# A decoder kernel on one Trainium2 core: setup moved into the fill, attention semaphores in two sets, and a reordered Mamba round

## The chip, the cores and the metric

The kernel runs on one core of one Trainium2 chip. The metric is the device time of one execution in microseconds (us); lower is better. The kernel before took 7854.28 us, the median of three runs (7828.51 to 7878.61).

The profile calls the engines PE (matrix multiply, with PEld for its weight loads), DVE (vector), ACT (scalar, activation functions), POOL (the second vector-like engine) and SP (which here issues DMAs). Every engine works through its own program in order and waits on semaphores that others raise.

## The reference, cut to what matters

The input `x` is 64 sequences of 128 tokens by 128 features (float32, 4.19 MB), with a context of 64 x 77 x 128 and a mask. Two decoder layers are computed in six stages: four Mamba layers, a cross attention, a mixture of experts, a trajectory step, a decoder block, and a last cross block. Some 45% of the time goes to the Mamba stage, which the change touches most. One of its layers computes

```
residual = hidden + residual;  h = layernorm(residual) * w + b
xin, z   = split(h @ in_w.T);  u = silu(causal_conv(xin) + cb)
dtr, B, C = split(u @ xp_w.T); dt = softplus(dtr @ dtp_w.T + dtp_b)
for each of 16 states n:  s_n[t] = exp(dt*A_n)[t] * s_n[t-1] + (dt*u*B_n)[t]
y = sum_n C_n * s_n + D*u;     hidden = (y * silu(z)) @ out_w.T
```

A is stored as a logarithm, so the kernel needs the exponential of it, negated (`a_neg`).

## The kernel before, in words

**Mamba stage** (`mamba_stage`, lines 97 to 763). The 64 sequences are 16 groups of four; a round does one group of one layer, so there are 64 rounds. A round runs three groups at once: the 16 scans of the present group, the last steps of the group behind (its gate, its output product, its new residual), and the first steps of the group ahead (norm, convolution, silu, projections, dt). Each round is one block of the five engine programs (line 594), which ends when all engines are through; two sets of semaphores take turns (`Turns`), and SP clears the other set at the start of a block.

*DVE* scans state after state: `dve_scan` (L422) needs the decay of that state from ACT and the input term `dBu` from POOL. The scan of a state read out on DVE (eleven of them) goes in place into PSUM, and `dve_read_out` (L439) multiplies it by C. For states 1, 5, 8, 10 and 13 the scan goes to plain memory (SBUF) and POOL reads it out (L450). Between scans DVE does the gate of the group behind after scan 1 (L337), the mean and variance of the group ahead after scan 3 (`Pre.dve`, L199 and L202), and three steps of softplus after scans 8, 9 and 11.

*ACT* makes the decays: `act_da(n+1, n)` writes the decay of state n+1 during step n, into one of two PSUM places that alternate with n; it waits until state n-1 has been scanned and read out. Each is a small column of zeros (L390) and two exponentials (L393). Between them stand, in this order: after the decay of state 3, the silu block (two silus of the convolution, L249, a wait for the gate, two silus of z, L319); after the decay of state 5, the copy of x's projection (`act_x`, L260) and of the new residual (`act_new`, L353); after the decay of state 6 the variance (`act_var`, L213 and L214); later softplus, the normalised tokens (L219) and their transposed copy (L231). Silu, exponential and logarithm are in different function tables, so a table load stands where the kind changes.

*PE* sums the read-out states into two PSUM banks by products with the identity (L467), which DVE's next read-out into the same buffer waits for. Its order at the start of a round:

```
behind.pe_late_sums; ahead.pe_conv(1); wait gate; sum(0); ahead.pe_z; sum(1); ahead.pe_x; behind.pe_out; sum(2); sum(3)
```

`pe_z` (L313) waits for the silus of the convolution, `pe_x` (L255) for those and for z's first silu, and `pe_out` (L343, L347) makes the residual that `act_new` copies.

*POOL* makes `dBu` (L408), two states ahead of the scan, and reads out its five states. *SP* loads rows of B and C, the residuals, and stores.

In a layer's first round (shape 0) DVE also copies `w_out` (L683) and builds the skip matrices (L495), and in its 15th (shape 14) it builds the next layer's convolution weights (L488 to L491).

**Before the first round** three blocks run one after the other. The first (L2844) issues 15 DMAs, 13 of them copies from DRAM to DRAM (the residual stream, its padding, a padded copy of `x`, of the context and of the mask), and waits for all. The second (L167) sets buffers to zero on DVE. The third (L507, the fill) loads the first weights, and runs the first steps for two groups.

**The attention stages** (`xattn_stage`, `trajectory_stage`, `decoder_stage`) run 19, 18 and 19 rounds, each a block. They have one set of semaphores (`Sems`): after each block SP clears it (L66) and a barrier of all engines follows (L67).

Of the kernel before, what the change touches and what calls it, by code (L numbers as in the profile page):

```python
# [16 lines left out]
P = 128  # L17
BATCH, SEQ, D = 64, 128, 128
GB = 4
# [17 lines left out]
LATE = 2  # L37
HCD = (2, 0, 1, 2, 0, 1, 2, 0, 1, 0, 1)
# [58 lines left out]
def mamba_stage(nc, w, consts, res, bc_dram):  # L97
# [9 lines left out]
    with ExitStack() as ctx:  # L107
# [26 lines left out]
        var, rstd, shift = (sb(n, [P, GB]) for n in ("var", "rstd", "shift"))  # L134
# [3 lines left out]
        ab, ey, ln1, small = (sb(n, [P, CH, TOK]) for n in ("ab", "ey", "ln1", "small"))  # L138
        dt, dtu, u, zg = (pair(n, [P, CH, TOK]) for n in ("dt", "dtu", "u", "zg"))
# [27 lines left out]
        with nc.Block() as block:  # L167
            @block.vector
            def _(dve):
                nc.vector.memset(h_ch[:], 0.0)  # L170
                nc.vector.memset(zeros[:], 0.0)
                nc.vector.memset(small_at[:], SMALL_Y)
                nc.vector.memset(poly_at[:], -0.75 * THIRD)
                nc.vector.memset(eps_at[:], LN_EPS)
                nc.vector.memset(xp[2 * DS:2 * DS + DR + 1, :], 1.0)
                nc.vector.memset(u[1][:], 0.0)
                nc.vector.memset(zg[1][:], 0.0)
                for part in hcd + hcp:
                    nc.vector.memset(part[:], 0.0)
                nc.vector.memset(w_out[:], 0.0)  # L180
                nc.vector.memset(bank[:, B_DA:8], 0.0)

        s = Turns(nc, ctx, ["mb_" + n for n in [
            "res", "rp", "store", "rows", "b0", "b1", "b2", "b3", "c0", "c1", "c2", "c3",
            "stats", "var", "norm", "xh", "tr", "h", "conv", "u", "xp", "xps", "dtp", "abs", "ey", "sq", "small", "ln", "poly", "log", "dt", "dtu", "z", "zg",
            "dbu", "da", "scan", "hcd", "hcp", "sumd", "sump", "late", "yg", "out", "new", "raw", "weights", "wb", "skip", "wo", "apos", "aneg"]])

        class Pre:
# [5 lines left out]
            def load(self, sp, g):  # L194
                sp.dma_start(r_tok[:], tile_rows(res, g)).then_inc(s["mb_res"], 16)
# [166 lines left out]
        class Scan:  # L362
# [17 lines left out]
            def act_da(self, act, m, j):  # L380
                q = self.q if m < DS else self.next_q
                n = m % DS
                if j >= 1:
# [6 lines left out]
                nc.scalar.activation(da_of(n)[:, :, 0:1], zeros[:], ACT.Copy)  # L390
                for c in range(CH):
                    k = c * DS + n
                    e = nc.scalar.activation(da_of(n)[:, c * GB:(c + 1) * GB, 1:],  # L393
# [17 lines left out]
            def dve_scan(self, dve, n):  # L411
# [10 lines left out]
                nc.vector.tensor_tensor_scan(flat(to), flat(da_of(n)), flat(dBu[n % RING][:]), 0.0,  # L422
# [62 lines left out]
        def dve_weights(dve):  # L485
            dve.wait_ge(s["mb_raw"], 5 * 16)
            for k in range(DC):
                nc.vector.tensor_tensor(w_conv[:, k, :], w_u[:], conv_row[:, k, :], ALU.mult)  # L488
            nc.vector.tensor_copy(w_x[:], x_raw[:])
            nc.vector.tensor_copy(conv_b[:], vec[:, CB:CB + CH])  # L490
            nc.vector.tensor_copy(norm_wb[:], vec[:, NW:NW + 2]).then_inc(s["mb_wb"], 1)  # L491

        def dve_skip(dve):
            for c in range(CH):
                m = nc.vector.tensor_scalar(skip[:, c], ident[:], vec[:, DD + c:DD + c + 1], None, ALU.mult)  # L495
            m.then_inc(s["mb_skip"], 1)
# [2392 lines left out]
```

## Time and profile before

| | |
|---|---|
| median of three runs | 7854.28 us |
| the profiled execution, its own time | 7862.71 us |
| its span, first to last instruction | 7860.9 us |
| mean granted TensorE clock in it | 0.841 |

| engine | busy us | share of the span |
|---|---|---|
| PE | 6285.0 | 80% |
| DVE | 6331.9 | 81% |
| ACT | 4396.8 | 56% |
| POOL | 4934.3 | 63% |

A share of busy time is an average over stages with different limits, so the stages are read one by one. The page cuts the span into 40 slices; in the first 19, some 3,730 us, which is the Mamba stage, DVE stands at 9 (90% or more) in all but the first slice, and the other engines below it or, POOL, beside it. A timeline lists instructions in order of time, with the idle time of the engine ahead of them and who ended it.

### The profile page before, as it was taken

The numbers are of one execution on the slowest core, as the hardware profiler recorded it, in microseconds if no ns is written. First come the engines' busy times: TensorE is split into PE (matmuls) and PEld (weight loads), VectorE is DVE, ScalarE is ACT, GpSimd is POOL, SyncE is SP. The second block draws the span as 40 slices with busy tenths as digits, with TensorE's granted clock in tenths as the row PEclk, the third lists the DMA queues.
The fourth block names the chain that finished last, engine by engine and source line by source line (L and its number), as shares of the span: only waits on it lengthen the run. The fifth ranks groups of instructions, "written<-read, shape, count | busy, mean of one in ns | idle before, by whom it ended". The sixth has DMA issues, their size and how long they took to land. (4 is left out here: it accounts for less than half of the span.)

```text
span 7860.9 us, 92400 instructions
## 1 busy us (share of the span) xinstructions
PE 6285.0 (80%) x25986; PEld 3332.1 (42%) x26001; DVE 6331.9 (81%) x14154; ACT 4396.8 (56%) x8495; POOL 4934.3 (63%) x3020
## 2 busy tenths in 40 slices
PE   5888888988888988888798777777557777777745
PEld 2333333333333333333455545555334554545522
DVE  4999999999999999999555488888666666666557
ACT  3666666766666666766455434444225555555533
POOL 4999999998999989999322176666123444344300
PEclk9999999999999999999767788888557777777755
DMA  4444444444444444434101077776110000000011
GB/s 169 172 158 171 164 167 154 173 155 164 165 159 170 159 176 156 173 156 168 50 22 28 18 231 220 223 216 197 45 34 11 7 9 10 10 10 10 7 38 35
DMA packets 373862, 896.52 MB, mean 114 GB/s; under 512 B 28169, under 2 KB 270214, under 8 KB 307110
## 3 DMA queue, kind: packets, MB, share of 16 engines
q1 hardware_dynamic: 332646, 692.64, 24.0%
q0 software_dynamic: 40960, 201.36, 8.9%
q14 instruction: 204, 1.67, 0.1%
q8 instruction: 52, 0.85, 0.0%
HBM read 850.57 MB, written 56.77 MB: 115 GB/s over the span
## 5 line engine op out<-in xcount | busy, mean ns | idle before, releaser
L408 POOL TENSOR_TENSOR mb_dBu<-mb_dtu,mb_rows_b 128x1024 f32<-128x1024 f32 x1026 | 2398.5, 2362 | 74.5 <-DVE mb_bank L422 41.0
L422 DVE TENSOR_TENSOR_SCAN mb_bank<-mb_bank,mb_dBu 128x1024 f32<-128x1024 f32 x704 | 1608.7, 2285 | 92.5 <-PEq L594 49.6
L467 PE MATMUL mb_bank<-mb_hcd,ident 128*128 128x512 f32 x2560 | 1232.0, 612 | 105.9 <-DVE mb_hcd L439 98.9
L393 ACT ACTIVATE mb_bank<-mb_dt,mb_a_neg 128x508 f32<-128x508 f32 x2050 | 1311.1, 670 | 1.5
L450 POOL TENSOR_TENSOR mb_hcp<-mb_hs,mb_rows_c 128x1024 f32<-128x1024 f32 x320 | 753.5, 2355 | 221.4 <-DVE mb_hs L422 221.4
L439 DVE TENSOR_TENSOR mb_hcd<-mb_bank,mb_rows_c 128x1024 f32<-128x1024 f32 x704 | 861.8, 1224 | 31.4
L467 PEld LDWEIGHTS mb_bank<-mb_hcd,ident 128*128 128x128 f32 x2560 | 474.1, 195 | 758.8 <-issue 509.0
L422 DVE TENSOR_TENSOR_SCAN mb_hs<-mb_bank,mb_dBu 128x1024 f32<-128x1024 f32 x320 | 729.6, 2280 | 0.0
L1588 POOL DMA_INDIRECT ex_rows<-in_ex_table,ex_idx x512 | 492.0, 961 | 330.7 <-issue 169.0
L467 PE MATMUL mb_bank<-mb_hcp,ident 128*128 128x512 f32 x1024 | 544.9, 659 | 140.2 <-POOL mb_hcp L450 139.3
L390 ACT ACTIVATE mb_bank<-mb_zeros 128x8 f32<-128x8 f32 x1025 | 176.0, 172 | 755.5 <-DVE mb_hcd L439 330.2
L1080 PE MATMUL de_bank<-ident,de_a_e 128*128 128x128 f32 (+1 forms) x2048 | 370.2, 340 | 211.0 <-DVE de_a_e L1196 210.9
L242 PE MATMUL mb_bank<-mb_h_ch,mb_w_conv 128*128 128x512 f32 x1048 | 474.2, 594 | 0.9 <-ACT mb_h_ch L231 0.9
L1037 POOL TENSOR_TENSOR de_a_e<-de_a_sp,de_a_m 128x1024 f32<-128x1024 f32 x128 | 245.0, 1914 | 332.9 <-DVE de_a_m L1182 179.5
L1080 PEld LDWEIGHTS de_bank<-ident,de_a_e 128*128 128x128 f32 (+1 forms) x2048 | 300.6, 180 | 264.6 <-DVE de_a_e L1196 239.7
L467 PEld LDWEIGHTS mb_bank<-mb_hcp,ident 128*128 128x128 f32 x1024 | 199.4, 202 | 435.0 <-issue 218.9
L1150 ACT ACTIVATE de_a_pt<-de_bank 128x512 f32<-128x512 f32 (+1 forms) x512 | 280.8, 591 | 122.6 <-PE de_bank L1080 122.5
L1182 DVE MAX8 de_a_m<-de_a_sp 128x8 f32<-128x128 f32 x1024 | 210.1, 277 | 143.7 <-ACT de_a_sp L1135 71.0
L1565 PE MATMUL ex_bank<-ex_w_sim,ex_xT 128*128 128x512 f32 x512 | 257.6, 644 | 80.9 <-PEq L67 74.4
L1672 ACT ACTIVATE ex_dg_in<-ident,ex_lin 128x128 f32<-128x128 f32 x512 | 156.5, 388 | 295.5 <-DVE ex_lin L1707 295.5
L242 PEld LDWEIGHTS mb_bank<-mb_h_ch,mb_w_conv 128*128 128x128 f32 x1048 | 198.8, 190 | 257.1 <-issue 255.8
L1642 PE MATMUL ex_bank<-ex_rows,ex_dg_in 128*128 128x256 f32 x1024 | 291.0, 448 | 0.0
(372 smaller groups left out, 12903.1 us busy)
## 6 DMA issues: line engine op xcount, KB each, us to landing
mb_rows_b<-bc_rows SPq DMA_DIRECT2D x259, 1024.0 KB, 7.0
mb_rows_c<-bc_rows SPq DMA_DIRECT2D x258, 1024.0 KB, 6.7
stream<-mb_r_post SPq DMA_DIRECT2D x69, 256.0 KB, 2.4
mb_r_tok<-stream SPq DMA_DIRECT2D x67, 256.0 KB, 2.7
mb_r_old<-stream SPq DMA_DIRECT2D x65, 256.0 KB, 2.8
ex_rows<-in_ex_table,ex_idx POOLq DMA_INDIRECT x512, 5.5
tj_x_tok<-stream SPq DMA_DIRECT2D x17, 256.0 KB, 3.0
bc_rows<-mb_xp SPq DMA_DIRECT2D x65, 64.0 KB, 2.1
```

What stands on the lines that cost most here:

```text
L242: m = nc.tensor.matmul(bank[:, M0 + c], w_conv[:, k, c * P:(c + 1) * P], h_ch[:, :, k:k + SEQ], start=(k == 0), stop=(k == DC - 1))
L393: e = nc.scalar.activation(da_of(n)[:, c * GB:(c + 1) * GB, 1:], dt[q][:, c].rearrange("p (b t) -> p b t", b=GB)[:, :, 1:], ACT.Exp, scale ...
L408: nc.gpsimd.tensor_tensor(by_c(dBu[m % RING][:]), by_c(chains(dtu[q][:])), over_c(rows_b[:, n]), ALU.mult).then_inc(s["mb_dbu"], 1)
L422: nc.vector.tensor_tensor_scan(flat(to), flat(da_of(n)), flat(dBu[n % RING][:]), 0.0, ALU.mult, ALU.add).then_inc(s["mb_scan"], 1)
L439: nc.vector.tensor_tensor(by_c(hcd[HCD[k]][:]), by_c(da_of(n)), over_c(rows_c[:, n]), ALU.mult).then_inc(s["mb_hcd"], 1)
L450: nc.gpsimd.tensor_tensor(by_c(hcp[(k + self.q) % 2][:]), by_c(hs[k % 2][:]), over_c(rows_c[:, n]), ALU.mult).then_inc(s["mb_hcp"], 1)
L467: m = nc.tensor.matmul(bank[:, B_Y + c], ident[:], part[:, c * GB:(c + 1) * GB], start=(n == 0), stop=False)
L1080: m = self.nc.tensor.transpose(self.bank[0:nk, 4 + j, h * P:(h + 1) * P], self.e_of(t, nk)[:, 4 * j + h], self.ident[:])
L1150: self.nc.scalar.activation(self.pt[t % 2][0:nk, 4 * j:4 * j + 4].rearrange("p h q -> p (h q)"), self.bank[0:nk, 4 + j], ACT.Copy).then_in ...
L1565: nc.tensor.matmul(bank[:, j], xT[q][:, b], w_sim[:, 4 * j:4 * j + 4], start=True, stop=True).then_inc(p["sim"], 1)
L1588: nc.gpsimd.indirect_dma_start(rowsb[b][:, h], None, w["table"], bass.IndirectOffsetOnAxis(idx[b][:, h:h + 1], 0)).then_inc(got[b], 16)
L1642: m = nc.tensor.matmul(bank[:, HID, 0:FI], dg_in[:, h], rowsb[k % GB][:, h, IB:IB + FI], start=False, stop=(h == PH - 1))
```

## The change

**Setup.** The first block keeps only two DMAs (identity and head mask). The other 13 are issued in the fill: four of them (`early`, 9.4 MB: the stream, its padding, `x`) behind the weight loads, nine (`late`, 4.0 MB) behind the load of the third group; the fill's end waits for all. The block of memsets is gone; DVE clears what is needed at the start of the fill, and the rest behind the convolution weights. The first groups are loaded from `x` itself. PE's first product, with a zeroed `u`, becomes one with a zeroed buffer, further back.

**Semaphores.** The three attention stages use `Turns`: SP clears the other set at the start of a block, and the clear and the barrier behind each block are gone. The decoder's loop of 13 rounds becomes one of six pairs, with one more round behind it.

**Norm statistics.** `Pre.dve` and `act_var` leave the rounds. ACT sums the four sequences in step 14 (four copies with a running sum, one small scaling) and, in step 0 of the next round, sums their squares about the mean (four squares, one small step).

**PE.** `pe_z` goes ahead of the wait for the gate and of `sum(0)`.

**Scan 4.** Its decay is made in step 2, ahead of the silu block, without a wait, into `ey` in SBUF; step 3 makes none.

**Weights.** `w_out`, the skip matrices and the small copies go to ACT (steps 5 and 9 of the rounds concerned); the convolution weights stay on DVE, in step 12, with one operand copied to PSUM by ACT (step 11).

```
+            def act_sums(self, act, there):
+                act.wait_ge(s["mb_res"], there)
+                for b in range(GB):
+                    m = nc.scalar.activation(xh[:, b], r_tok[:, b], ACT.Copy, accum_out=sums[:, b:b + 1])
+                m.then_inc(s["mb_sums"], 1)
+                act.wait_ge(s["mb_sums"], 1)
+                nc.scalar.activation(shift[:], sums[:], ACT.Copy, scale=-1.0 / D).then_inc(s["mb_mean"], 1)
+            def act_squares(self, act):
+                for b in range(GB):
+                    m = nc.scalar.activation(xh[:, b], r_tok[:, b], ACT.Square, bias=shift[:, b:b + 1],
+                                             accum_out=squares[:, b:b + 1])
+                m.then_inc(s["mb_squares"], 1)
+                act.wait_ge(s["mb_squares"], 1)
+                nc.scalar.activation(var[:], squares[:], ACT.Identity, bias=eps_at[:, 0:1], scale=1.0 / D).then_inc(s["mb_var"], 1)
...
             def act_da(self, act, m, j):
-                if j >= 1:
+                if m == EARLY:
+                    pass
+                elif j >= 1:
...
+                da = early_da if n == EARLY else da_of(n)
...
             def _(act):
-                        scan.act_da(act, n + 1, n)
+                        if n + 1 != EARLY:
+                            scan.act_da(act, n + 1, n)
                         if n == 2:
+                            scan.act_da(act, EARLY, n)
                             for c in range(CH):
                                 ahead.act_conv(act, c, 1)
...
-                        if n == 5:
-                            pre.act_var(act)
+                        if n == 0:
+                            pre.act_squares(act)
+                        if n == 5 and shape == 0:
+                            act.wait_ge(s["mb_out"], 1)
+                            nc.scalar.activation(w_out[:], out_raw[:], ACT.Copy).then_inc(s["mb_wo"], 1)
+                            act_skip(act)
...
+                        if n == 14:
+                            pre.act_sums(act, 16)
...
             def _(dve):
-                        if n == 6 and shape == 0:
-                            nc.vector.tensor_copy(w_out[:], out_raw[:]).then_inc(s["mb_wo"], 1)
-                        if n == 6 and shape == GROUPS - 2:
-                            dve.wait_ge(s["mb_xp"], 1)
-                            dve_weights(dve)
-                        if n == 6 and shape == 0:
-                            dve_skip(dve)
-                        if n == 3:
-                            pre.dve(dve)
+                        if n == 12 and shape == GROUPS - 2:
+                            dve.wait_ge(s["mb_wu"], 1)
+                            dve_weights(dve, bank[:, M1, 0:DI])
...
             def _(pe):
                     behind.pe_late_sums(pe)
                     ahead.pe_conv(pe, 1)
+                    ahead.pe_z(pe)
                     pe.wait_ge(s["mb_yg"], 1)
                     scan.pe_sum(pe, 0)
-                    ahead.pe_z(pe)
                     scan.pe_sum(pe, 1)
...
             @block.sync
             def _(sp):
-                pre.load(sp, 1)
+                pre.load(sp, x_in, 0)
                 load_raw(sp, 0)
                 load_used(sp, 0)
+                moves = early(sp, s["mb_moved"])
                 sp.wait_ge(s["mb_xh"], 1)
...
+                moves += late(sp, s["mb_moved"])
...
+                sp.wait_ge(s["mb_moved"], 16 * moves)
...
 # in each of the three attention stages
-        s = Sems(nc, st, [...])
+        s = Turns(nc, st, [...])
         def round_of(i, shape):
+            s.use(shape % 2)
                 def _(sp):
+                    s.clear_other()
-            s.clear()
```

## Rows read from the trace of the kernel before

**Rows 1.** Busy us (instructions) of PE, PEld, DVE, ACT, POOL; clock; DMA share; GB/s.
```profile
1000.00:2000.00 1000.00, 883.83 (x2120) 366.39 (x2118) 963.91 (x692) 668.54 (x1224) 913.99 (x421) 0.96 0.42 161
```

**Rows 2.** DVE timeline of two rounds: start, duration, instruction, idle before it.
```profile
2000.10 2.30 DVE L422 TENSOR_TENSOR_SCAN mb_bank<-mb_bank,mb_dBu 128x1024 f32<-128x1024 f32 x1 [0.69 <-PEq L594]
...
2015.68 2.30 DVE L422 TENSOR_TENSOR_SCAN mb_bank<-mb_bank,mb_dBu 128x1024 f32<-128x1024 f32 x1 [0.54 <-ACT mb_bank L393]
...
2021.35 2.27 DVE L422 TENSOR_TENSOR_SCAN mb_bank<-mb_bank,mb_dBu 128x1024 f32<-128x1024 f32 x1
...
2056.57 2.30 DVE L422 TENSOR_TENSOR_SCAN mb_bank<-mb_bank,mb_dBu 128x1024 f32<-128x1024 f32 x1 [0.76 <-PEq L594]
...
2070.28 0.86 DVE L199 BATCH_NORM_STATS2 mb_stats<-mb_r_tok 128x6 f32<-128x128 f32 x4
...
2071.52 2.27 DVE L422 TENSOR_TENSOR_SCAN mb_bank<-mb_bank,mb_dBu 128x1024 f32<-128x1024 f32 x1
...
2077.16 2.27 DVE L422 TENSOR_TENSOR_SCAN mb_bank<-mb_bank,mb_dBu 128x1024 f32<-128x1024 f32 x1
```

**Rows 3.** ACT timeline of the same two rounds.
```profile
2019.38 1.28 ACT L393 ACTIVATE mb_bank<-mb_dt,mb_a_neg 128x508 f32<-128x508 f32 x2
...
2042.32 1.65 ACT L219 ACTIVATE mb_xh<-mb_r_tok,mb_shift,mb_rstd 128x128 f32<-128x128 f32 x4 [2.29 <-POOL mb_shift L209]
...
2052.38 0.18 ACT L390 ACTIVATE mb_bank<-mb_zeros 128x8 f32<-128x8 f32 x1 [2.05 <-DVE mb_hcd L439]
...
2060.16 0.18 ACT L390 ACTIVATE mb_bank<-mb_zeros 128x8 f32<-128x8 f32 x1 [2.23 <-DVE mb_hcd L439]
...
2062.36 0.18 ACT L390 ACTIVATE mb_bank<-mb_zeros 128x8 f32<-128x8 f32 x1 [0.80 <-DVE mb_hs L422]
...
2063.77 1.28 ACT L249 ACT_TABLE_LOAD   x1
...
2074.22 0.60 ACT L353 ACTIVATE mb_r_post<-mb_bank 128x512 f32<-128x512 f32 x1 [1.30 <-PE mb_bank L347]
```

**Rows 4.** PE timeline of the same two rounds.
```profile
2000.11 3.25 PE L331 MATMUL mb_bank<-mb_hcp,ident 128*128 128x512 f32 x4 [2.12 <-PEq L594]
...
2056.62 1.96 PE L331 MATMUL mb_bank<-mb_hcp,ident 128*128 128x512 f32 x4 [2.24 <-PEq L594]
...
2063.56 1.91 PE L467 MATMUL mb_bank<-mb_hcd,ident 128*128 128x512 f32 x4
2065.81 1.99 PE L313 MATMUL mb_bank<-mb_h_ch,mb_w_z 128*128 128x512 f32 x4 [0.33 <-ACT mb_u L249]
2067.63 1.88 PE L467 MATMUL mb_bank<-mb_hcp,ident 128*128 128x512 f32 x4
```

**Rows 5.** POOL timeline of the second of these rounds.
```profile
2064.72 11.62 POOL L408 TENSOR_TENSOR mb_dBu<-mb_dtu,mb_rows_b 128x1024 f32<-128x1024 f32 x5
```

**Rows 6.** DVE timeline, work on weights: in the fill, then beside POOL in rounds.
```profile
66.11 1.43 DVE L488 TENSOR_TENSOR mb_w_conv<-mb_w_u,mb_conv_row 128x256 f32<-128x256 f32 x4 [3.27 <-DMA mb_conv_row<-in_mb_conv_row]
...
1053.21 1.54 DVE L683 COPY mb_w_out<-mb_out_raw 128x256 f32<-128x256 f32 x1
1054.67 2.58 DVE L495 TENSOR_SCALAR mb_skip<-ident,mb_vec 128x128 f32<-128x128 f32 x2
...
3668.37 3.48 DVE L488 TENSOR_TENSOR mb_w_conv<-mb_w_u,mb_conv_row 128x256 f32<-128x256 f32 x4 [1.42 <-DMA mb_conv_row<-in_mb_conv_row]
```

**Rows 7.** Timeline of the start, DVE and SP (SPq issues DMAs).
```profile
46.12 0.49 DVE L170 MEMSET mb_h_ch<- 128x524 f32 x1 [45.25 <-PEq L2844]
...
58.69 0.40 SPq L195 DMA_DIRECT2D mb_r_tok<-stream  x1
...
117.96 2.30 DVE L422 TENSOR_TENSOR_SCAN mb_bank<-mb_bank,mb_dBu 128x1024 f32<-128x1024 f32 x1 [13.73 <-PEq L507]
```

**Rows 8.** SP's releases by a block's end (L1343) and the barrier (L67), 3776 to 3791.
```profile
L1343 SPq EVENT_SEMAPHORE  x1: 17/17/17, 3786.6 to 3786.6; - x1
...
L67 SPq EVENT_SEMAPHORE  x2: 17/17/17, 3778.9 to 3787.0; - x2
```

More of the change, by code:

```diff
@@ L133, in mamba_stage @@
         mv = sb("mv", [P, GB, 2])
-        var, rstd, shift = (sb(n, [P, GB]) for n in ("var", "rstd", "shift"))
+        var, rstd, shift, sums, squares = (sb(n, [P, GB]) for n in ("var", "rstd", "shift", "sums", "squares"))
         xh = sb("xh", [P, GB, D])
@@ L165, in mamba_stage @@
         y_psum, x_psum = bank[:, B_Y:B_Y + CH], bank[:, M0:M0 + CH]
[L167 to L181, printed above, removed]
         s = Turns(nc, ctx, ["mb_" + n for n in [
             "res", "rp", "store", "rows", "b0", "b1", "b2", "b3", "c0", "c1", "c2", "c3",
-            "stats", "var", "norm", "xh", "tr", "h", "conv", "u", "xp", "xps", "dtp", "abs", "ey", "sq", "small", "ln", "poly", "log", "dt", "dtu", "z", "zg",
-            "dbu", "da", "scan", "hcd", "hcp", "sumd", "sump", "late", "yg", "out", "new", "raw", "weights", "wb", "skip", "wo", "apos", "aneg"]])
+            "init", "blank", "moved", "stats", "sums", "mean", "squares", "var", "norm", "xh", "tr", "h", "conv", "u", "xp", "xps", "dtp", "abs", "ey", "sq", "small", "ln", "poly", "log", "dt", "dtu", "z", "zg",
+            "dbu", "da", "scan", "hcd", "hcp", "sumd", "sump", "late", "yg", "out", "new", "raw", "weights", "copies", "wu", "wb", "skip", "wo", "apos", "aneg"]])
         class Pre:
@@ L580, in _ @@
                 first.pe_dt(pe, False)
+                pe.wait_ge(s["mb_blank"], 1)
+                for c in range(CH):
+                    nc.tensor.matmul(bank[:, B_Y + c], ident[:], hcd[HCD[-1]][:, c * GB:(c + 1) * GB], start=True, stop=False)
                 first.pe_dt(pe, True)
@@ L1515, in experts_stage @@
         p = Prefixed(s, "ex_")
-        got = [st.enter_context(nc.semaphore(f"ex_got{b}")) for b in range(GB)]
+        got = consts["got"]
         w_sim = sb("w_sim", [P, 2 * PH, NK])
@@ L2463, in _ @@
                             n4.dve_done(dve)
-            s.clear()
         for i in (-2, -1, 0):
             round_of(i, i)
-        with nc.Fori(1, GROUPS - 2) as i:
-            round_of(i, 1)
-        for i in range(GROUPS - 2, GROUPS + 1):
+        with nc.Fori(0, (GROUPS - 4) // 2) as pairs:
+            for q in range(2):
+                round_of(pairs * 2 + 1 + q, 1 + q)
+        for i in range(GROUPS - 3, GROUPS + 1):
             round_of(i, i)
+        s.clear()
 def decoder_host(i):
@@ L2843, in build @@
         loaded = st.enter_context(nc.semaphore("consts_loaded"))
+        consts["got"] = [st.enter_context(nc.semaphore(f"ex_got{b}")) for b in range(GB)]
         with nc.Block() as block:
@@ L2862, in _, with early, late @@
                 nc.vector.memset(consts["half_neg"][:], -0.5)
[L2863 removed]
+        def early(sp, sem):
+            copies = [(after_mamba, a["x"]), (padded[0:TOK], a["x"][0:TOK]), (padded[TOK * (GROUPS + 1):], a["x"][0:3 * TOK]),
+                      (x_ahead[0:BATCH * SEQ], a["x"])]
+            for dst, src in copies:
+                sp.dma_start(dst, src).then_inc(sem, 16)
+            return len(copies)
+        def late(sp, sem):
+            copies = [(stream[k][TOK * GROUPS:], a["x"][0:TOK]) for k in range(1, 5)]
+            copies += [(x_ahead[BATCH * SEQ:], a["x"][0:TOK])]
+            for whole, src in ((ctx_ahead, a["ctx"]), (mask_ahead, a["mask"])):
+                copies += [(whole[0:BATCH], src), (whole[BATCH:], src[0:GB])]
+            for dst, src in copies:
+                sp.dma_start(dst, src).then_inc(sem, 16)
+            return len(copies)
+        mamba_stage(nc, of("mb"), consts, a["x"], padded, bc_dram, early, late)
         xattn_stage(nc, of("xa"), consts, x_ahead, padded[TOK:TOK * (GROUPS + 2)], ctx_ahead, mask_ahead, stream[1][0:TOK * GROUPS])
```

91 lines of the change are left out of this document (56 added, 35 removed).

## The prediction, made before the changed kernel was run

> **What bounds the kernel now.** I read the page's 40 slices first: in the Mamba slices DVE is full. The windows view confirms it for one stretch: DVE is busy 964 of 1,000 us, POOL 914, at a granted clock of 0.96 [rows 1]. Then I read the DVE timeline of two neighbouring rounds [rows 2]. DVE runs without a gap, with two exceptions: about 0.7 us at the start of a round, and in one round of two 0.54 us ahead of scan 4, which the trace puts down to ACT's decay. So what DVE no longer does is worth its time only as far as the next decay is there. I therefore followed the decays on ACT [rows 3] and, behind them, PE's order [rows 4]. Times below are from a round's first scan; the plain round starts at 2056.57, the stalled one at 2000.10.
>
> **The round: what is taken off DVE.** From the norm's first row to scan 4 is 2071.52 - 2070.28 = 1.24 us, which goes; the 0.54 us stall in every second round goes too, since scan 4's decay is early. Scan 4 could start at 13.71. If nothing else held DVE that would be 1.24 + 0.27 = 1.51 us a round.
>
> **The round: what ACT and PE do instead.** The new sums and squares cover four tiles of 128x128; the nearest row, four tokens' normalisation, is 1.65 us [rows 3]. The running sum's own price isn't in the trace: I bound it by 0 and by a doubling to 3.3, and take the lower end, nearest to the row. Either way it lies in ACT's waits: 2.23 us ahead of the second decay, 2.05 us ahead of the last decay of a round, with 0.8 us more ahead of the third decay. Without that cover it would cost up to 1.9 us each. The added waits on its own two semaphores hold only the next decay, inside the same gaps.
>
> The early decay is another matter. It stands in front of the silu block, behind decay 3, whose start to the table load is 2063.77 - 2062.36 = 1.41 us. That is what one more decay adds. z's product now starts at 2065.81 - 2056.57 = 9.24; it becomes 9.24 + 1.4 = 10.64. PE has meanwhile nothing to do: the convolution ends at about 7.0 (start of sum 0, 2063.56), and sum 0, which filled this gap, now stands behind z. Sum 0 takes 1.81 (sum 1's start less z's is 1.82 for the same number of passes). From z's start to the start of the residual's copy is 2074.22 - 2065.81 = 8.41 us, through sum 1, x's projection and the output product. With sum 0 added, that copy starts at 10.64 + 8.41 + 1.81 = 20.86 instead of 17.65.
>
> **Who waits for it.** ACT is in order: the decay for scan 6 stands behind that copy, 0.60 + 1.28 = 1.88 us later. So scan 6 cannot start before 20.86 + 1.88 = 22.74. It starts now at 2077.16 - 2056.57 = 20.59 in the plain round and at 21.25 in the stalled one, where DVE itself was the limit. So **scan 6 becomes the stall**: +2.15 and +1.49, mean +1.82 us a round, after DVE has given up everything that the norm gave it. Behind scan 6 the work is unchanged in order and amount on all engines (softplus hangs on the same PE chain and shifts with it), so nothing is paid back: 64 x 1.82 = +116 us.
>
> **The clock.** In the stalled round PE's first group takes 3.25 us where the plain one takes 1.96 [rows 4]: the half level (1.2 GHz) after 2.12 us of idleness; after 2.24 us in the other round it did not fall. PE now idles 10.64 - 7.0 = 3.6 us ahead of z, and what follows is the chain to scan 6. The price per round lies between 0 and 2 x 1.29 (z and sum 0 both at half rate). I take 1.29 in every second round, as often as the slow group comes now: 64 x 0.65 = +42 us.
>
> **Scan 4's operands.** Its decay and its `dBu` are now both in SBUF. The trace shows what such work costs beside POOL [rows 6]: four products take 1.43 us in the fill and 3.48 us in a round; a copy takes 1.54, two scalings 2.58. POOL runs five `dBu` back to back from 8.15, 2.32 us each [rows 5], so one ends at 8.15 + 3 x 2.32 = 15.11; if scan 4 has to wait for that, it starts 1.40 late and ends at 17.4, and scan 5 ends by 20.9, still ahead of 22.74. The stall covers it: 0. POOL would lose 2.3 us there, and its next `dBu`, for scan 7, is then ready at 19.8, in time. The Trainium skill ("SBUF — State Buffer", section "Who interferes with whom") says that a DVE instruction with two SBUF inputs and a GpSimd instruction that reads SBUF lock each other out for the whole instruction, which speaks against this step; by that rule the forecast's sum stays as it is, and only the third rival's changes.
>
> **Special rounds.** In a layer's first round 1.54 + 2.58 = 4.1 us leave DVE; in its 15th 1.42 of waiting and 3.48, against 1.43 that come back in step 12 (one operand in PSUM, so at the fill's price): 3.5. Both lie behind scan 6, so they count in full: 4 x 7.6 = -30 us. ACT's share (some 1 us) has its slack ahead of decays 7 and 13.
>
> **The fill.** The first scan starts at 117.96; the fill's first issue stands at 58.69, after 46 us of copies and the memsets [rows 7]. The copies moved 13.4 MB (sizes in the code), so 0.30 MB per us. After, the fill starts at about 4 us, an estimate from the two small loads that remain. By its own steps it would end at 4 + 59 = 63, a gain of 55. But the queue holds 9.4 MB from about 9.5, so to 41; the store of B and C's rows queues behind it, then five row loads of 1 MB and 4.0 MB late: 41 + 9.3/0.30 = 72, and 3 to land: 75. SP's wait for the late copies holds the end of the block and so all engines. I take -43 us, from -55 (hidden) to -28 (if everything late waits for the last row).
>
> **Semaphore sets.** From a block's release to the barrier's is 3787.0 - 3786.6 = 0.4 us [rows 8]; with 56 rounds, three clears staying, 53 x 0.4 = -21. SP's clear at the start delays loads that are needed a round later: 0. The decoder's longer loop body I put at 0: the trace doesn't price it, and the other two stages already have loops of pairs. Bounds -25 and 0.
>
> **Sum.** +116 + 42 - 30 - 43 - 21 = +64. Against the profiled execution, 7862.7, that gives 7927; its own time stands 8.4 above the median of the runs, 7854.3, so the forecast is **7918 us**, +0.8%.
>
> **Rivals.** (A) PE stays at full clock: without the 42, +22, so 7876. For it: the 2.24 us gap that did nothing. (B) PE falls in every round: 64 x 1.29 = 83 instead of 42, +105, so 7959; for it, the new gap is longer than either of those seen. With two slow groups it would be +188, 8042, the far end. (C) **Faster**: the residual's copy does not catch scan 6, and DVE's relief sets the round. It decides at a copy that starts by about 17.5 (scan 6 would come at 13.71 + 5.64 = 19.35, less 1.88). Then 64 x 1.51 = -97, in all -191: 7663. With scan 4 held by POOL for 1.40 each round it is -101: 7753. DVE's work on weights shows such waits [rows 6], so I put C at 7753. It is also what the rule of the Trainium skill named above would give. Against C: PE's program puts sum 0 and sum 1, 3.6 us, between z and that copy, and 20.86 is over 3 us late. That the change doesn't do what it says has no place apart: the norm's DVE instructions are simply gone.
>
> **Chances.** Forecast 0.42, A 0.21, B 0.23, C 0.14. A measurement of this kernel tells about 1% (79 us) from no change: faster means under 7776, slower over 7933. C gives 0.14 faster. Of the forecast, with the fill's and the sets' bounds (about 40 us either way), 0.4 lies above 7933, and of B 0.8: 0.17 + 0.18, slower 0.35; the rest, 0.51, within 1%. The range leaves out C and the far end of B, and reaches from A less the fill's bound to B plus the sets': 7820 to 8010. The likeliest case alone is 7880 to 7960.
>
> **What would show it.** DVE's timeline: no norm rows, scan 4 between 13.7 and 15.2, and scan 6 at 22.5 to 24, its idle ended by ACT's decay (L393's line); the residual's copy near 20.9, its idle ended by PE's output product; z at 10.6 with PE idle ahead of it; rounds of 58 us and more. The first scan near 75. If scan 6 comes at 19.4 to 20.7 without idle, C holds, and the in-order reading of ACT or PE is wrong. If scan 4 lasts 2.3 us with its start at 13.7, the lock does not touch it.

## The result and the profile after

The changed kernel takes **7938.63 us** (median of 7 runs, 7907.57 to 7962.75) against 7854.28 (7 runs beside it): the ratio is **1.0108**, 95% interval 1.0077 to 1.0138. It is slower, 20.6 us above the forecast and inside the range. The profiled execution took 7962.26 us, with a span of 7960.0, 99.1 more than before.

Where the 99.1 us are, by the span's stages: the fill saves 44.75 (first scan at 73.21, before 117.96), the Mamba rounds take 163.6 more (first scan to last instruction, 3650.1 to 3813.7), and the attention stages save 20.6 (cross attention +13.0, the trajectory stage -6.6, the decoder -27.0). The last 0.9 us lie in the other stages and between stages.

The windows view of the kernel after, same columns and same stretch as [rows 1], and the page's first line:

```profile
1000.00:2000.00 1000.00, 849.53 (x2029) 349.60 (x2029) 915.84 (x521) 688.76 (x1446) 907.13 (x402) 0.96 0.39 153
```
```profile
PE 6311.9 (79%) x25986; PEld 3329.5 (42%) x26001; DVE 6321.1 (79%) x13608; ACT 4597.7 (58%) x9561; POOL 5057.2 (64%) x3020
```

DVE was 964 us busy in these 1,000 and is 916 now, since a round takes longer; its work has hardly become less. Over the whole span its busy time fell from 6331.9 us to 6321.1 only: the norm and the weights freed some 109 us, and the scans take 87 us more, about 80 of them in scan 4, as the next rows show. The DVE timeline of a round at full clock, first scan at 2333.96, answers to the second half of [rows 2]: scan 0, scans 4 and 5, and scan 6.

```profile
2333.96 2.30 DVE L428 TENSOR_TENSOR_SCAN mb_bank<-mb_bank,mb_dBu 128x1024 f32<-128x1024 f32 x1 [1.05 <-PEq L622]
...
2347.68 3.57 DVE L428 TENSOR_TENSOR_SCAN mb_bank<-mb_ey,mb_dBu 128x1024 f32<-128x1024 f32 x1
...
2352.42 2.28 DVE L428 TENSOR_TENSOR_SCAN mb_hs<-mb_bank,mb_dBu 128x1024 f32<-128x1024 f32 x1
2356.59 2.30 DVE L428 TENSOR_TENSOR_SCAN mb_bank<-mb_bank,mb_dBu 128x1024 f32<-128x1024 f32 x1 [1.90 <-ACT mb_bank L398]
```

Scan 4 starts 13.72 after scan 0 and waits for nothing that the profile names, but lasts 3.57 us, where it lasted 2.27. Scan 6 comes at 22.63, behind 1.90 us of idleness that ACT's decay ends. Now ACT and PE in the same round, answering to [rows 3] and [rows 4]: the squares, the early decay into `mb_ey`, the table load behind it, the residual's copy; z ahead of sum 0.

```profile
2335.20 0.39 ACT L212 ACTIVATE mb_xh<-mb_r_tok,mb_shift 128x128 f32<-128x128 f32 x1
2335.49 0.19 ACT L212 ACTIVATION_READ_ACCUMULATOR mb_xh<-mb_r_tok,mb_shift 128x1 f32 x1
...
2337.55 0.18 ACT L395 ACTIVATE mb_bank<-mb_zeros 128x8 f32<-128x8 f32 x1 [0.39 <-DVE mb_hcd L445]
...
2341.18 1.31 ACT L398 ACTIVATE mb_ey<-mb_dt,mb_a_neg 128x508 f32<-128x508 f32 x2
2342.51 1.28 ACT L251 ACT_TABLE_LOAD   x1
...
2354.68 0.60 ACT L355 ACTIVATE mb_r_post<-mb_bank 128x512 f32<-128x512 f32 x1 [2.25 <-PE mb_bank L349]
```
```profile
2344.55 1.98 PE L315 MATMUL mb_bank<-mb_h_ch,mb_w_z 128*128 128x512 f32 x4 [1.72 <-ACT mb_u L251]
2346.37 1.88 PE L473 MATMUL mb_bank<-mb_hcd,ident 128*128 128x512 f32 x4
2348.09 1.88 PE L473 MATMUL mb_bank<-mb_hcp,ident 128*128 128x512 f32 x4
```

In another round (first scan at 1321.58) PE has waited 3.47 us ahead of z. The granted clock of the four microseconds behind that wait is 0.50, the half level of 1.2 GHz (windows view, columns as in [rows 1]); z takes 3.78 us, sum 0 3.08, the copy starts at 23.68, and scan 6 at 25.59 after 4.82 us of idleness:

```profile
1332.16 3.78 PE L315 MATMUL mb_bank<-mb_h_ch,mb_w_z 128*128 128x512 f32 x4 [3.47 <-ACT mb_u L251]
1335.74 3.08 PE L473 MATMUL mb_bank<-mb_hcd,ident 128*128 128x512 f32 x4
...
1338.66 1.88 PE L473 MATMUL mb_bank<-mb_hcp,ident 128*128 128x512 f32 x4
```
```profile
1332.00:1336.00 4.00, 3.83 (x5) 1.77 (x6) 3.96 (x3) 1.30 (x4) 4.00 (x3) 0.50 0.00 0
```
```profile
1347.17 2.30 DVE L428 TENSOR_TENSOR_SCAN mb_bank<-mb_bank,mb_dBu 128x1024 f32<-128x1024 f32 x1 [4.82 <-ACT mb_bank L398]
```

At the start, SP and DVE, answering to [rows 7]: the first group's load, the last of the late copies, the first scan.

```profile
3.46 0.38 SPq L181 DMA_DIRECT2D mb_r_tok<-in_x  x1
...
61.03 1.50 SPq L2914 DMA_DIRECT2D mask_ahead<-in_mask  x2
```
```profile
73.21 2.30 DVE L428 TENSOR_TENSOR_SCAN mb_bank<-mb_bank,mb_dBu 128x1024 f32<-128x1024 f32 x1 [21.98 <-PEq L516]
```

### The profile page after: what moved, and what is told of

Same layout as the page of the kernel before. It is cut to its first block and busy times, and to the rows that moved or that the text cites. A ratio compares the mean times of both kernels' runs of the same rounds, so it can differ in the third digit from the quotient of the medians.

```text
span 7960.0 us, 92226 instructions
## 1 busy us (share of the span) xinstructions
PE 6311.9 (79%) x25986; PEld 3329.5 (42%) x26001; DVE 6321.1 (79%) x13608; ACT 4597.7 (58%) x9561; POOL 5057.2 (64%) x3020
## 5 line engine op out<-in xcount | busy, mean ns | idle before, releaser
L413 POOL TENSOR_TENSOR mb_dBu<-mb_dtu,mb_rows_b 128x1024 f32<-128x1024 f32 x1026 | 2520.7, 2479 | 101.4 <-DVE mb_bank L428 59.7
L428 DVE TENSOR_TENSOR_SCAN mb_bank<-mb_bank,mb_dBu 128x1024 f32<-128x1024 f32 x640 | 1464.6, 2288 | 266.4 <-ACT mb_bank L398 185.4
L398 ACT ACTIVATE mb_bank<-mb_dt,mb_a_neg 128x508 f32<-128x508 f32 x1922 | 1230.0, 671 | 1.5
L473 PE MATMUL mb_bank<-mb_hcp,ident 128*128 128x512 f32 x1024 | 494.5, 605 | 103.8 <-POOL mb_hcp L456 103.8
L315 PE MATMUL mb_bank<-mb_h_ch,mb_w_z 128*128 128x512 f32 x260 | 169.7, 786 | 175.5 <-ACT mb_u L251 175.5
L1081 POOL TENSOR_TENSOR de_a_km<-de_kT,hmask 128x308 f32<-128x308 f32 x64 | 64.4, 1006 | 374.2 <-PE de_bank L1096 374.1
```

The lines of the kernel that those rows point to most:

```text
L398: e = nc.scalar.activation(da[:, c * GB:(c + 1) * GB, 1:], dt[q][:, c].rearrange("p (b t) -> p b t", b=GB)[:, :, 1:], ACT.Exp, scale=a_neg ...
L413: nc.gpsimd.tensor_tensor(by_c(dBu[m % RING][:]), by_c(chains(dtu[q][:])), over_c(rows_b[:, n]), ALU.mult).then_inc(s["mb_dbu"], 1)
L428: nc.vector.tensor_tensor_scan(flat(to), flat(da), flat(dBu[n % RING][:]), 0.0, ALU.mult, ALU.add).then_inc(s["mb_scan"], 1)
L473: m = nc.tensor.matmul(bank[:, B_Y + c], ident[:], part[:, c * GB:(c + 1) * GB], start=(n == 0), stop=False)
```

## The experiments

My theory: of the parts in the rounds, the two changes of order cost the time (z ahead of sum 0, scan 4's decay ahead of the silu block), through the chain PE, residual's copy, decay of scan 6; the clock adds to it; the rest of the change gains. The rivals were that the norm statistics on ACT, or the lock between DVE and POOL, make the rounds longer.

In the table, "round" is the mean length of the 52 ordinary rounds (all but a layer's first, 15th and 16th), and scan 4, scan 6 and the residual's copy are typical starts in a round, all in us from the profile of each kernel. The ratio, with its 95% interval, is to runs of the kernel before that were made beside that kernel; their medians lie between 7831.94 and 7863.23 us, so kernels are compared by their ratios.

| kernel | median us | ratio | round | scan 4 | scan 6 | copy |
|---|---|---|---|---|---|---|
| before | 7854.28 | | 56.21 | 14.95, 15.58 | 20.59, 21.25 | 17.65 |
| after | 7938.63 | 1.0108 (1.0077 to 1.0138) | 59.11 | 13.71 | 22.63 | 20.72 |
| z_back | 7787.43 | 0.9906 (0.9871 to 0.9941) | 56.54 | 13.71 | 20.92 | 19.00 |
| decay_back | 7853.93 | 0.9990 (0.9965 to 1.0016) | 57.48 | 14.55 | 21.28 | 19.37 |
| both_back | 7768.50 | 0.9896 (0.9864 to 0.9928) | 55.90 | 14.55 | 20.22 | 17.65 |
| z_alone | 7901.83 | 1.0063 (1.0041 to 1.0086) | 57.49 | 14.95 | 21.28 | 19.37 |
| busy_pe | 7896.50 | 1.0058 (1.0037 to 1.0078) | 58.25 | | 22.63 | |
| norm_back | 7764.61 | 0.9870 (0.9829 to 0.9911) | 56.20 | 14.95 | 20.58 | |
| best | 7857.49 | 1.0014 (0.9995 to 1.0033) | 57.64 | 13.71 | 19.37 | 17.31 |
| best_norm | 7948.90 | 1.0094 (1.0063 to 1.0126) | 58.85 | 14.94 | 20.58 | |

**The two changes of order.** `z_back` is the kernel after with z behind sum 0 again:

```
                     ahead.pe_conv(pe, 1)
-                    ahead.pe_z(pe)
                     pe.wait_ge(s["mb_yg"], 1)
                     scan.pe_sum(pe, 0)
+                    ahead.pe_z(pe)
```

> The changed kernel with one edit undone: z's product stands behind sum 0 again. Theory 1 (in-order chain: scan 6 waits for ACT's decay, which stands behind the residual's copy, which waits for PE's output product): the copy comes 1.8 us earlier, at about 18.9 instead of 20.7 from the round's start, scan 6 at 20.7 to 20.9 (then scan 5's end is the limit, as scan 4 still lasts 3.6), the plain round 56.2 to 56.6 instead of 58.1, and PE's gap ahead of z is half as long, so few or no slow groups there: 7938 less 118 to 180, so 7760 to 7820. Theory 2 (the lock between scan 4 and POOL costs the time): scan 4 and POOL are as before, so rounds stay near 58 and the time at 7900 or more.

`decay_back` keeps z ahead and makes scan 4's decay as the others are, in PSUM, behind the silu block (`da_of(n)` in place of `early_da`, in the scan too):

```
-                        if n + 1 != EARLY:
-                            scan.act_da(act, n + 1, n)
+                        scan.act_da(act, n + 1, n)
                         if n == 2:
-                            scan.act_da(act, EARLY, n)
```

> The changed kernel with one edit undone: scan 4's decay is made behind the silu block, in PSUM; z stays ahead of sum 0. Theory 1: z starts 1.4 us earlier, at 9.2, the residual's copy at about 19.4, scan 6 at 21.3 to 21.4 with 1 us of idle ahead of it, the plain round about 56.8: 7938 less 80 to 130, so 7810 to 7860. Theory 2: with the lock gone scan 4 lasts 2.3, scan 6 comes at 20.2 without idle, rounds of 55.6, and the time is about 7710.

`both_back` has both edits.

> The changed kernel with both edits undone: z behind sum 0, scan 4's decay behind the silu block in PSUM. Theory 1: the residual's copy at 17.65 in the plain round as before the change, scan 4 at 14.6 behind its decay (0.8 idle), scan 6 at about 20.2 without idle, plain round 55.4; where PE starts slow, the stall at scan 4 comes back (15.6) and the round is 56.4: a mean gain of 0.2 to 0.5 us a round over the kernel before, with the special rounds, the fill and the sets 7735 to 7765. Theory 2 gives the same here. If the running sums on ACT cost time in the round (a third theory), it stays above 7800.

`z_alone` is the other way about: the kernel before, with `ahead.pe_z(pe)` ahead of the wait for the gate and of `sum(0)`, and nothing else.

> The kernel before with one edit of the change alone: z's product ahead of sum 0. Theory 1 (in-order chain through the residual's copy): the copy comes 1.8 us later, at about 19.4, and scan 6 at 21.3 instead of 20.6, as in the run with the decay put back; rounds of 57.1 and, where PE is slow behind its gap, more: about 7850 plus 60 to 90, so 7910 to 7940. A rival (this edit is free or gains the 0.54 us stall of every second round, and only the early decay costs): 7830 to 7850.

DVE in `z_back` (scan 4, scan 6; first scan at 2232.77), in `decay_back` (first scan at 2271.45), in `both_back` (scans 4, 5 and 6; first scan at 2266.91) and in `z_alone` (scan 6; first scan at 2324.83):

```profile
2246.48 3.57 DVE L428 TENSOR_TENSOR_SCAN mb_bank<-mb_ey,mb_dBu 128x1024 f32<-128x1024 f32 x1
...
2253.69 2.30 DVE L428 TENSOR_TENSOR_SCAN mb_bank<-mb_bank,mb_dBu 128x1024 f32<-128x1024 f32 x1 [0.18 <-ACT mb_bank L398]
```
```profile
2286.00 2.30 DVE L426 TENSOR_TENSOR_SCAN mb_bank<-mb_bank,mb_dBu 128x1024 f32<-128x1024 f32 x1 [0.75 <-ACT mb_bank L396]
...
2292.73 2.30 DVE L426 TENSOR_TENSOR_SCAN mb_bank<-mb_bank,mb_dBu 128x1024 f32<-128x1024 f32 x1 [0.98 <-ACT mb_bank L396]
```
```profile
2281.47 2.30 DVE L426 TENSOR_TENSOR_SCAN mb_bank<-mb_bank,mb_dBu 128x1024 f32<-128x1024 f32 x1 [0.76 <-ACT mb_bank L396]
...
2284.94 2.28 DVE L426 TENSOR_TENSOR_SCAN mb_hs<-mb_bank,mb_dBu 128x1024 f32<-128x1024 f32 x1
2287.14 2.27 DVE L426 TENSOR_TENSOR_SCAN mb_bank<-mb_bank,mb_dBu 128x1024 f32<-128x1024 f32 x1
```
```profile
2346.11 2.30 DVE L422 TENSOR_TENSOR_SCAN mb_bank<-mb_bank,mb_dBu 128x1024 f32<-128x1024 f32 x1 [0.61 <-ACT mb_bank L393]
```

The idleness ahead of scan 6 is 1.90 us with both, 0.98 with z ahead alone, 0.18 with the early decay alone, and none with neither. By the ratios, z ahead costs 0.9% while the decay is late (0.9896 to 0.9990; on the kernel before, 0.6%), and 2.0% beside the early decay (0.9906 to 1.0108). The early decay costs 1.2% while z is ahead, and nothing that can be told (0.9896 against 0.9906, the intervals overlap) while sum 0 fills PE's gap. The two delays of the copy simply add: the early decay's 1.35 us (17.65 to 19.00) and z's 1.72 (to 19.37) make 3.07 (20.72). Time is lost only by what reaches scan 6 as a wait, so the second delay costs more than the first. Undoing both takes 2.1% off: the theory stands, and what remains of the change makes the kernel 1.0% faster. Two sizes were missed: `z_alone` took less than the 7910 to 7940 us expected, though clearly more than the rival's 7830 to 7850, and `both_back` came out just above its range.

**The clock.** `busy_pe` is the kernel after with two of the convolution's four products of the second half made twice, so that PE's wait ahead of z, up to 3.5 us in ordinary rounds, is at most 1.8 us in 61 of the 64 rounds:

```
+                    for k in range(2):
+                        nc.tensor.matmul(bank[:, 1], w_conv[:, k, P:2 * P], h_ch[:, :, k:k + SEQ], start=(k == 0), stop=(k == 1))
                     ahead.pe_conv(pe, 1)
                     ahead.pe_z(pe)
```

> The changed kernel with two products of the convolution made twice, in the gap in which PE waits for the silus, so that PE idles 1.8 instead of 3.6 us there. Theory 1 with the clock as a second cost: z keeps its place at 10.6, the copy at 20.7, scan 6 at 22.6 in nearly every round, and the 25 rounds in which scan 6 waited longer (62 us more in all in the profiled execution) become plain ones: 7938 less 40 to 60, so about 7880 to 7900, still slower than the kernel before. If those longer waits are not from PE's clock after its idleness, the time stays at 7938 or grows by what PE does more.

PE in `busy_pe` (first scan at 2302.10) and its scan 6:

```profile
2307.36 1.88 PE L739 MATMUL mb_bank<-mb_h_ch,mb_w_conv 128*128 128x512 f32 x4
2309.08 3.60 PE L244 MATMUL mb_bank<-mb_h_ch,mb_w_conv 128*128 128x512 f32 x8
2312.68 1.99 PE L315 MATMUL mb_bank<-mb_h_ch,mb_w_z 128*128 128x512 f32 x4
```
```profile
2324.73 2.30 DVE L428 TENSOR_TENSOR_SCAN mb_bank<-mb_bank,mb_dBu 128x1024 f32<-128x1024 f32 x1 [1.88 <-ACT mb_bank L398]
```

More work for PE, and less time: the ratio falls from 1.0108 to 1.0058, 0.5% or 39 us, and scan 6 stands at 22.63 in nearly every round. In the kernel after, 25 of 64 rounds have 3.3 to 4.8 us of idleness ahead of scan 6; what they have above the usual 1.9 sums to 62 us, and 3 such rounds remain here. Those 25 are among the 31 rounds in which PE has waited 3.3 us or more ahead of z; behind the other six of these waits, and behind the 33 waits of 2.0 us or less, z ran at full rate. These 33 are rounds in which PE's first group was slow already (2.98 us in the round at 2333.96), so that the convolution ended later and the wait became shorter. The length of the wait alone thus doesn't tell whether the clock falls. In `decay_back` PE waits 2.0 to 2.1 us ahead of z in 40 rounds, and z was slow (2.9 to 3.7 us) in 20 of them: part of what z ahead costs by itself is the clock, too.

**The lock.** `pool_holds` is the kernel after, in which POOL begins the `dBu` of scan 6 only when scan 4 is done, so nothing on POOL reads SBUF beside scan 4:

```
-                    pool.wait_ge(s["mb_scan"], m - RING + 1)
+                    pool.wait_ge(s["mb_scan"], 5 if m == 6 else m - RING + 1)
```

> The changed kernel, with POOL's product for scan 6 waiting until scan 4 is done, so that POOL stands idle when scan 4 starts. If scan 4's 3.57 us are a wait for POOL's running instruction plus 2.29 of work, it lasts 2.3 now, and scan 5 ends 1.3 earlier; scan 6 stays at 22.6, since it waits for ACT, and the time stays at 7938. If two SBUF operands make the scan itself slower, it stays at 3.57. If the lock had a part in scan 6's wait, rounds fall below 58 and the time to 7860.

DVE's scan 4 and scan 6 in `pool_holds` (first scan at 2329.72):

```profile
2343.43 2.29 DVE L428 TENSOR_TENSOR_SCAN mb_bank<-mb_ey,mb_dBu 128x1024 f32<-128x1024 f32 x1
...
2352.35 2.30 DVE L428 TENSOR_TENSOR_SCAN mb_bank<-mb_bank,mb_dBu 128x1024 f32<-128x1024 f32 x1 [3.17 <-ACT mb_bank L398]
```

The same scan of the same two SBUF operands takes 2.29 us without POOL and 3.57 beside it, and the 1.28 us saved there stand again ahead of scan 6 (3.17 for 1.90). The time is 7945.33, ratio 1.0108 (1.0075 to 1.0140): the wait of scan 4 for POOL is real and cost the changed kernel nothing.

**The norm statistics.** `norm_back` is `both_back` with the statistics on DVE and the variance on ACT in step 5, as before; the sums and squares on ACT leave the rounds:

```
                         if n == 3:
+                            pre.dve(dve)
...
-                        if n == 0:
-                            pre.act_squares(act)
-                        if n == 14:
-                            pre.act_sums(act, 16)
```

> The kernel with both edits undone, and the norm's statistics on DVE again in the rounds (rows behind scan 3, variance on ACT in step 5). Theory 1: scan 4 was waiting for its decay at 14.55, so DVE's 1.24 us of statistics fill most of that wait: scan 4 at 14.95, round 56.1 instead of 55.7 in plain rounds, no change in slow ones: 7768 plus 15 to 30, so 7780 to 7800. If what DVE no longer does is worth its full 1.24 us a round: 7768 plus 79, so about 7847.

The round grows by 0.30 us, as expected, and the Mamba stage of the profile by 14.6, but the total doesn't show it: 7764.61 lies below the 7780 to 7800 expected and below `both_back`, and the intervals overlap. Moving the statistics buys next to nothing here.

**The attention stages' sets.** `xa_one_set` is `both_back` with cross attention on one set, a clear and a barrier behind each block (`Sems` for `Turns`, no `use` or `clear_other`, `s.clear()` in the loop); `xa_after` is the same edit on the kernel after, and `xa_before` gives cross attention alone two sets in the kernel before.

```
-        s = Turns(nc, st, ["xa_" + n for n in [
+        s = Sems(nc, st, ["xa_" + n for n in [
...
-            s.use(shape % 2)
...
-                    s.clear_other()
...
+            s.clear()
```

> The kernel with both edits undone, and the cross attention's semaphores in one set again, with the clear and the barrier behind each block. If a release costs 0.4 us, as the trace of before shows, the cross attention takes 7 us more than with two sets (733 in the run with both edits undone, 720 to 724 in the others), so 727 to 741. A rival, from the stages' times (710 before the change, 720 to 734 with two sets): the two sets themselves made this stage slower, and it comes back to about 710.

> The changed kernel with the cross attention's semaphores in one set again. If two sets are what lengthens this stage: it takes 668 to 711 us, as in the three runs with one set, instead of 719 to 734, as in the seven with two, and less of it lies at the half clock level (285 to 392 us instead of 443 to 476); the whole about 7938 less 15 to 50. If the stage's time only depends on when it starts: anywhere between 668 and 734.

> The kernel before, with two sets of semaphores in the cross attention alone. If two sets are what lengthens this stage: 719 to 734 us instead of 710, with 440 us or more of it at the half level, and the whole 10 to 20 us longer than before. If a clear and a barrier less simply saves 0.4 us a round, as predicted: 703.

Totals: 7755.92, ratio 0.9867 (0.9832 to 0.9901); 7947.09, ratio 1.0150 (1.0114 to 1.0187); 7862.01, ratio 1.0040 (1.0019 to 1.0061). The stage itself took 695.8, 681.9 and 701.6 us, against 710.1 before and 723.1 after. It fits no theory of the sets: one set spans 668 (`z_alone`) to 710, two sets 682 (`best`) to 734 (`both_back`). What goes along with the stage's length is the time that PE spends in it at the half level: 285 us in `z_alone`, 392 before, 449 after, 476 in `both_back`. The windows of the stage, before and after (columns as in [rows 1]), show the same instruction counts at a granted clock of 0.72 and 0.69:

```profile
3771.00:4482.00 711.00, 610.68 (x4608) 397.25 (x4608) 380.71 (x1237) 372.00 (x768) 194.94 (x240) 0.72 0.10 26
```
```profile
3890.00:4613.00 723.00, 632.47 (x4608) 409.93 (x4608) 381.46 (x1237) 371.70 (x768) 194.79 (x240) 0.69 0.09 25
```

In `xa_one_set` and `xa_after` the stage is 38 and 41 us shorter than in the kernels that they change, but the decoder, whose code is the same, is 35 and 27 us longer (1714.5 for 1679.4, 1705.9 for 1679.2), and the whole span changed by +4 and -9 us only. Whether the sets move the clock stays open, and so does why the whole of `xa_before` is 0.4% longer than the kernel before beside it.

**An attempt at the gain.** `best` is `z_back` with `pool_holds`' wait and with sum 1 behind the output product, to keep the early scan 4 and give scan 6 its decay in time; `best_norm` puts the statistics back on DVE, as in `norm_back`.

```
                     behind.pe_out(pe)
+                    scan.pe_sum(pe, 1)
```

> The changed kernel with three edits that follow from the runs so far: z behind sum 0, sum 1 behind the output product, and POOL's product for scan 6 waiting for scan 4. Theory 1: the residual's copy comes at about 17.2 instead of 19.0 (z behind sum 0), scan 4 lasts 2.3, scan 6 starts at 19.4 without idle, DVE is the bound again, and the plain round is 54.5 to 54.9 instead of 56.5: 7787 less 100 to 130, so 7660 to 7690. If another wait takes the place (POOL, whose work now starts 3 us later, for scans 7 to 9, or PE's sums), the round is 55.5 or more and the time 7730 or more.

> The same kernel with the norm's statistics on DVE again. Theory 1 (an engine's relief is worth what the next wait leaves of it): here no wait follows, so the statistics cost their full 1.24 us a round, scan 4 at 14.95 and scan 6 at 20.6: 64 x 1.24 = 79 us more than the kernel without them, against 0.3 us a round between the two runs before. If it is again 0.3 us a round, some other wait holds the round.

`best` came out 170 to 200 us above what theory 1 gave; the other case of the expectation, another wait in its place, is what came. Scan 4 at 13.71, the copy at 17.31 and scan 6 at 19.37 came as expected, and yet the round is 57.64. DVE (scan 8, the next round's scan 0 and its scan 14), ACT and POOL in `best`, in a round from 2279.83:

```profile
2307.63 2.29 DVE L428 TENSOR_TENSOR_SCAN mb_hs<-mb_bank,mb_dBu 128x1024 f32<-128x1024 f32 x1 [1.43 <-ACT mb_bank L398]
...
2336.88 2.30 DVE L428 TENSOR_TENSOR_SCAN mb_bank<-mb_bank,mb_dBu 128x1024 f32<-128x1024 f32 x1 [1.33 <-PEq L622]
...
2388.17 2.30 DVE L428 TENSOR_TENSOR_SCAN mb_bank<-mb_bank,mb_dBu 128x1024 f32<-128x1024 f32 x1 [0.87 <-ACT mb_bank L398]
```
```profile
2304.20 1.03 ACT L279 ACTIVATE mb_ab<-mb_bank 128x1024 f32<-128x1024 f32 x1 [3.49 <-PE mb_bank L274]
```
```profile
2295.91 6.98 POOL L413 TENSOR_TENSOR mb_dBu<-mb_dtu,mb_rows_b 128x1024 f32<-128x1024 f32 x3 [3.27 <-DVE mb_bank L428]
...
2331.86 4.67 POOL L413 TENSOR_TENSOR mb_dBu<-mb_dtu,mb_rows_b 128x1024 f32<-128x1024 f32 x2
```

The wait costs POOL 3.27 us; from 2295.91 it works without a break to 2336.53 (2331.86 + 4.67) and ends the round 1 us behind DVE, whose last instruction ends at 2335.55. POOL is last in 23 of the 52 ordinary rounds, and in none is it through before 56.67 us from the first scan, so that no round is shorter than 57.0 us. In the other 29, as in the next round here, DVE ends later still, behind 0.87 us of idleness ahead of scan 14; these rounds take 58.04 us in the mean. In all 52 ACT's softplus block waits for PE, and scan 8 for the decay behind it (1.43 us). The two edits weren't run apart, so their shares stay open. That POOL ends 0.3 us behind DVE is no sign of a limit by itself: it does so in every ordinary round of the kernels before, after and `both_back`, where it has first waited for DVE's scan 10 (1.32 us in the round at 2333.96 of the kernel after, 0.92 in the one shown of `both_back`), so that its end moves with DVE's.

`best_norm` is 91 us slower than `best` (79 expected): there the statistics do show. Scan 4 stands at 14.94 instead of 13.71, so POOL, which waits for it, idles 4.48 us for 3.27; scan 6 stands at 20.58 instead of 19.37, and the round is 1.21 us longer.

## Why the prediction was right, point by point

**The chain to scan 6** was right. z came at 10.58 (10.64 predicted), the residual's copy at 20.72 (20.86), scan 6 at 22.63 (22.74), with its idleness ended by the decay. The ordinary rounds without a longer wait there are 58.06 to 58.49 long, 2.0 us more than the mean before; 1.82 was predicted. Scan 6 itself comes 1.72 us later than the mean before. The other 0.31 us lie behind it, where the prediction had the work unchanged: from scan 6 to the next round's first scan it is 35.62 us instead of 35.31, and half of that is a wait of scan 10 for ACT's decay, which the kernel before doesn't have (DVE, same round):

```profile
2371.88 2.29 DVE L428 TENSOR_TENSOR_SCAN mb_hs<-mb_bank,mb_dBu 128x1024 f32<-128x1024 f32 x1 [0.15 <-ACT mb_bank L398]
```

Over 64 rounds the chain thus cost some 130 us instead of 116. The experiments undo the two causes one by one, and the idleness ahead of scan 6 goes with them.

**DVE's relief** was right in that scan 4 stands at 13.71 without a stall, and that nothing is gained by it. But the prediction took the 1.51 us as within reach if nothing else held DVE, and in no run did nothing else hold it. `both_back` has scan 6 at 20.22 without idleness and a round of 55.90, only 0.31 below before: scan 4 waits for its late decay again, 1.14 us in the mean. `z_back`, with the early scan 4 held by POOL and scan 6 at 20.92, is nearest to rival C with that hold: 7787 us, where C had 7753. C's 7663, without the hold, no run reached: in `best`, where scan 4 lasts 2.3 us and scan 6 stands at 19.37, POOL and ACT's decays made the round longer.

**The clock** was right in kind and mis-sized: +42 us predicted, as 1.29 in every second round. It came in 25 of 64 rounds, but z and sum 0 both slowed (3.78 for 1.98, 3.08 for 1.88), about 2.5 us each, 62 us in all. `busy_pe` took 39 us back. Rival B's term, 83 us for one slow group in every round, was as far off on the other side. What the forecast had wrong is the pattern: fewer rounds, each at nearly the double price (2 x 1.29) that it named as the upper bound.

**Special rounds**: the relief of 30 us came, though the round means hide it. A layer's first rounds grew from 59.68 to 60.90, the 15th fell from 61.38 to 60.04, and the 16th grew from 59.51 to 63.38 (the last round of all, counted to its last instruction, from 64.35 to 66.04). The ordinary rounds explain 52 x 2.90 = 151 of the 163.6 us, so these 12 added some 13 where the relief was forecast to cancel their part (12 x 2.47 - 30 = 0). But seven of the 25 long waits ahead of scan 6 fall into them, with 18 of the 62 us. Take these off, and the 2.0 us of the chain in each of the 12, and some 30 us of relief are left; this is an estimate from the round means. At the boundary of 1020.95 the last round of one layer and the first of the next both have the long wait ahead of scan 6 (DVE timeline, after):

```profile
982.23 2.30 DVE L428 TENSOR_TENSOR_SCAN mb_bank<-mb_bank,mb_dBu 128x1024 f32<-128x1024 f32 x1 [4.58 <-ACT mb_bank L398]
...
1047.35 2.30 DVE L428 TENSOR_TENSOR_SCAN mb_bank<-mb_bank,mb_dBu 128x1024 f32<-128x1024 f32 x1 [4.82 <-ACT mb_bank L398]
```

The first rounds of the later layers are alike at 61.65 to 62.02 us, where the very first, without it, takes 58.09. So the clock fell on these rounds more often than on others; the prediction had spread it evenly. The Mamba stage as a whole grew by 163.6 for a predicted 116 + 42 - 30 = 128.

**Scan 4's operands**: 0 predicted, 0 measured. Scan 4 and its wait ended at 17.3 (17.4 predicted), covered by the stall. POOL lost 2.0 us there (2.3 predicted): its five products behind 8.16 take 13.58 us for the 11.62 of [rows 5], and this was covered too. The rule of the Trainium skill ("SBUF — State Buffer", section "Who interferes with whom") is borne out by this trace for a scan with two SBUF inputs: 3.57 us beside POOL, 2.29 without.

```profile
2342.12 13.58 POOL L413 TENSOR_TENSOR mb_dBu<-mb_dtu,mb_rows_b 128x1024 f32<-128x1024 f32 x5
```

**Squares and sums on ACT**: 2335.20 to the small step's end is 1.96 us, with four reads of the accumulator of 0.19 each between the squares. Between one row's price and its double, it came near the lower end, and ACT still idles 0.39 us ahead of the second decay, for 2.23 before. The cover held.

**The fill**: 43 us predicted, 44.75 measured, by the step named: the late copies are issued up to 62.5, and SP's wait for the last of them, 9.9 us long, ends the fill.

**The sets**: 21 us predicted, 20.6 measured, in part by chance. The trajectory stage takes 283.5 to 284.5 us in every kernel with two sets and 290.2 to 292.2 with one, so its -6.6 belong to the sets (0.37 us for each of 18 rounds; 0.4 predicted). Cross attention's +13 and the decoder's -27 aren't shown to: with the same sets such a stage varies more than that from kernel to kernel (the decoder with two sets takes 1676 to 1715 us).

**The sum**: the step mis-sized is the Mamba rounds, 163.6 us for 128, by some 14 in the chain and 20 in the clock, of the same sign; the fill and the sets are within 2. The forecast is nearer to the median than that, 20.6 us low, by luck: the profiled execution stands 23.6 above the median of its runs, where the forecast took off the 8.4 of the kernel before.

## What to carry to other kernels

An engine that is busy 96% of a stretch is not worth relieving until the next limit is known: here these were ACT's decays and, once they came in time (`best`), POOL's chain. A step that is put ahead on an in-order engine delays all that stands behind it, so follow the last of these to its consumer. Two such moves delayed one copy by the sum of their delays, and the time went up by more than the sum of what each costs alone, because the first delay had used up the slack and because the gap that they opened on PE was followed by the half level. What pays of this change is what `both_back` keeps (7768.5 us, 1.0% faster than before): the setup in the fill, the weights off DVE, and the two sets in the trajectory stage. For the other two attention stages a gain by the sets isn't shown.

## What the runs showed of the hardware that was not expected

- A running sum on ACT is an instruction of its own in the trace: ACTIVATION_READ_ACCUMULATOR, 0.19 us behind each 128x128 square of 0.39.
- The DVE scan with both inputs in SBUF, started while a POOL product runs, takes 1.28 us longer, and the trace books that as busy time, not as idle time.
- In the kernel after, 25 of 31 waits of PE of 3.3 us or more ahead of z were followed by a slow z (granted clock 0.50 in the round shown), and none of 33 waits of 2.0 us or less was (z 1.98 in the round shown). In `decay_back` 20 of 40 waits of 2.0 to 2.1 us were. Filling the gap with repeated products made the kernel 0.5% faster.
- Cross attention with the same instructions took 668 to 734 us in different kernels, along with its time at the half level, 285 to 476 us.
